# Slot feed-forward: weight units loaded in the order of use, the second bias copied by GpSimd, group outputs sent on the queue of the weight units

## The chip, the cores and the metric

The kernel runs on one core of a Trainium2 chip. The metric is the time of one execution on the device in microseconds; the median of three runs stands for a kernel. Lower is better.

## The reference

Two transformer-like layers run on a batch of B=32 sequences of T=96 tokens (64 image patches and 32 text tokens) of width D=192. Each layer is an attention and a feed-forward, both with residuals. The part that matters here is the feed-forward of layer 0, a mixture over 64 slots: every sequence is gathered into 64 slot vectors, each slot has its own two-layer network with its own weights, and the results are spread back over the tokens.

```python
y = jnp.einsum('btd,bst->bsd', xn, dispatch_w)            # [32, 64, 192]
y = jnp.einsum('sio,bsi->bso', fc1_weight, y) + fc1_bias  # [64, 192, 768] weights
y = jax.nn.gelu(y, approximate=False)
y = jnp.einsum('sio,bsi->bso', fc2_weight, y) + fc2_bias  # [64, 768, 192] weights
out = jnp.einsum('bsd,bst->btd', y, combine_w)            # 64 slots back to 96 tokens
```

All weights are float32. The slot weights alone are 64 x 192 x 768 x 2 values, 75.5 MB, and each is used once, for 32 rows.

## The kernel before

The program is a row of stages, each a `Block` in which the five engines run their own instruction lists, with a barrier at the end: patch embedding, attention 0, slot dispatch, slot feed-forward (`slot_ffn`, L910), combine (L1064), then the second layer. The slot feed-forward, where the change lies, runs at about 342 to 550 us.

**Groups and units.** The 64 slots are worked in NGR=8 groups of GS=8 slots. A group's weights come in PER=4 units of 2304 KB: parts 0 and 1 hold its first-layer weights, parts 2 and 3 its second-layer weights. A unit fills one of NU=6 places of a ring (`g.ring`, 18432 bytes in each of 128 partitions). `load_unit` (L257) loads unit u, which is part `u % 4` of group `u // 4`, into place `u % 6`. The first six units (group 0 complete, and parts 0 and 1 of group 1) are loaded long before, during attention 0.

**TensorE** runs `first(0)`, and then for each group gr: `turn(gr)`, `first(gr+1)`, `second(gr)`. `first` (matmuls of L1028, 96 of them) waits for parts 0 and 1 of its group; `turn` (L1041) transposes the hidden rows; `second` (L1053, 2 x 48 matmuls) waits for part 2 and then for part 3. So TensorE takes the units in the order of groups 0 first, 1 first, 0 second, 2 first, 1 second, and so on. ACT and DVE copy the hidden rows out of PSUM (`evacuate`, L955 and L985), DVE adds the first bias (L992), ACT does the Gelu (L961), and DVE copies a group's output to the two-deep tile `y2g` (`y_copy`, L1001).

**SP** loads units 6 to 31 in the order of their numbers (L938 to L945). Before the load of unit u it waits until the unit that had the place six earlier has been used: `s_h1` counts the halves of `first`, `s_y2p` those of `second`. After unit 6 it also issues one transfer of the second bias, which broadcasts `fc2_b` over the batch into partitions 64 to 127 of `g.y2` (L945): 64 x 32 rows of 192 floats.

**ACT** also issues the group outputs (`put`, L963 to L967): after `y_copy(gr)` two transfers of 96 KB move `y2g` (128 partitions x 192 floats each) to four partitions of `g.y2` of 32 x 192 floats each. `y_copy(gr)` waits until the two transfers of group gr-2 have landed. The stage ends when the last of them has landed, since ACT waits for `s_y2` and the barrier waits for ACT; the combine stage's first matmul (L1080) reads `g.y2`.

Of the kernel before, what the change touches and what calls it, by code (L numbers as in the profile page):

```python
# [24 lines left out]
B = 32  # L25
T_IMG, T_TXT = 64, 32
T = T_IMG + T_TXT
D = 192
# [17 lines left out]
NS = 64  # L46
F = 768
FC = F // 128
GS = 8
NGR = NS // GS  # L50
SC = 4
SH = NS // 2
KQ = D // 64
UNIT = 2 * KQ * F
NU = 6
PER = 4
# [198 lines left out]
    g.b1_rows = hi["b"][64:66, :]  # L255


def load_unit(sp, A, g, u):

    gr, part = u // PER, u % PER  # L260
    src = A["slot_w1"][2 * gr + part] if part < 2 else A["slot_w2"][2 * gr + part - 2]
    sp.dma_start(g.ring[u % NU], src).then_inc(g.s_ring[u % NU], 16)

# [646 lines left out]
def slot_ffn(nc, A, g):  # L910


    with ExitStack() as ctx:
        def sem(name):
            return g.phase_sem("f_" + name)

        def sb(name, shape, dt=F32):
            return ctx.enter_context(nc.sbuf_tensor("f_" + name, shape, dt))

        NCK = 2 * FC  # L920
        N2 = F // 2
        hid = sb("hid", [128, 2, F])
        hT = sb("hT", [128, 2, NCK, 128])
        b1 = sb("b1", [128, NGR, NCK, SC])
        y2g = sb("y2g", [128, 2, 2, D])
        s_b1, s_b2, s_h1, s_hid_a, s_hid_v, s_hTp, s_hb, s_gelu, s_y2p, s_y2s = (
            sem(n) for n in ("b1", "b2", "h1", "hid_a", "hid_v", "hTp", "hb", "gelu", "y2p", "y2s"))
        s_y2 = [sem(f"y2_{i}") for i in range(2)]
        b_h = [[g.ps[:, 2 * n + r, 0:N2] for r in range(2)] for n in range(2)]
        b_hT = [g.ps[:, 4 + q, :] for q in range(3)]  # L930
        b_y = [g.ps[:, 7, r * D:(r + 1) * D] for r in range(2)]
        block = ctx.enter_context(nc.Block())

        @block.sync
        def _(sp):
            sp.dma_start(b1[:, :, :, :], A["slot_b1"].rearrange("p (g k c) -> p g k c", g=NGR, k=NCK)).then_inc(s_b1, 16)
            for u in range(NU, NGR * PER):
                gr, part = (u - NU) // PER, (u - NU) % PER  # L938
                if part < 2:
                    sp.wait_ge(s_h1, 2 * gr + 2)  # L940
                else:
                    sp.wait_ge(s_y2p, 2 * gr + part - 1)
                load_unit(sp, A, g, u)
                if u == NU:
                    sp.dma_start(g.y2[NS:2 * NS, :, :], A["fc2_b"].unsqueeze(1).broadcast_to([NS, B, D])).then_inc(s_b2, 16)  # L945
            sp.wait_ge(s_b2, 16)

        @block.scalar
        def _(act):
            def evacuate(gr):  # L950
                for n in range(2):
                    act.wait_ge(s_h1, 2 * gr + n + 1)
                    if gr >= 1:
                        act.wait_ge(s_hTp, 3 * gr)
                    act.activation(hid[:, 0, n * N2:(n + 1) * N2], b_h[n][0], ACT.Copy).then_inc(s_hid_a, 1)  # L955

            def gelu(gr):
                for q in range(3):
                    act.wait_ge(s_hb, 3 * gr + q + 1)
                    piece = hT[:, gr % 2, 4 * q:4 * q + 4, :]  # L960
                    act.activation(piece, piece, ACT.Gelu).then_inc(s_gelu, 1)  # L961

            def put(gr):  # L963
                act.wait_ge(s_y2s, gr + 1)
                for r in range(2):
                    s0 = SH * r + SC * gr
                    act.dma_start(g.y2[s0:s0 + SC, :, :], y2g[:, gr % 2, r, :]).then_inc(s_y2[gr % 2], 16)  # L967

            evacuate(0)
            for gr in range(NGR):  # L970
                gelu(gr)
                if gr + 1 < NGR:
                    evacuate(gr + 1)
                put(gr)
            for i in range(2):
                act.wait_ge(s_y2[i], 32 * NGR // 2)

        @block.vector
        def _(v):
            def evacuate(gr):  # L980
                for n in range(2):
                    v.wait_ge(s_h1, 2 * gr + n + 1)
                    if gr >= 1:
                        v.wait_ge(s_hTp, 3 * gr)
                    v.tensor_copy(hid[:, 1, n * N2:(n + 1) * N2], b_h[n][1]).then_inc(s_hid_v, 1)  # L985

            def add_bias(gr):
                for q in range(3):
                    v.wait_ge(s_hTp, 3 * gr + q + 1)
                    if gr >= 2:  # L990
                        v.wait_ge(s_y2p, 2 * (gr - 1))
                    v.tensor_tensor(hT[:, gr % 2, 4 * q:4 * q + 4, :].rearrange("p k (c b) -> p k c b", c=SC),  # L992
                                    b_hT[q].rearrange("p (k c b) -> p k c b", k=4, c=SC),
                                    b1[:, gr, 4 * q:4 * q + 4, :].unsqueeze(3).broadcast_to([128, 4, SC, B]),
                                    ALU.add).then_inc(s_hb, 1)

            def y_copy(gr):
                v.wait_ge(s_y2p, 2 * gr + 2)
                if gr >= 2:
                    v.wait_ge(s_y2[gr % 2], 32 * (gr // 2))  # L1000
                v.tensor_copy(y2g[:, gr % 2, :, :], g.ps[:, 7, 0:2 * D].rearrange("p (r d) -> p r d", r=2)).then_inc(s_y2s, 1)  # L1001

            v.wait_ge(s_b1, 16)
            evacuate(0)
            for gr in range(NGR):
                add_bias(gr)
                if gr + 1 < NGR:
                    evacuate(gr + 1)
                y_copy(gr)

        @block.tensor
        def _(pe):
            def landed(u):
                pe.wait_ge(g.s_ring[u % NU], 16 * (u // NU + 1))

            def first(gr):
                landed(PER * gr)
                landed(PER * gr + 1)
                w1 = [g.ring[(PER * gr + i) % NU].rearrange("p (c k f) -> p c k f", c=2, k=KQ) for i in range(2)]
                if gr >= 1:  # L1020
                    pe.wait_ge(s_hid_a, 2 * gr)
                    pe.wait_ge(s_hid_v, 2 * gr)
                for n in range(2):
                    for k in range(KQ):
                        for c in range(SC):
                            for r in range(2):
                                rows = slice(64 * r, 64 * r + 64)
                                mm = pe.matmul(b_h[n][r][B * c:B * (c + 1), :], g.yT[rows, k, SC * gr + c, :],  # L1028
                                               w1[c // 2][rows, c % 2, k, n * N2:(n + 1) * N2],
                                               start=(k == 0), stop=(k == KQ - 1), tile_position=(64 * r, B * c))  # L1030
                    mm.then_inc(s_h1, 1)

            def turn(gr):
                pe.wait_ge(s_hid_a, 2 * gr + 2)
                pe.wait_ge(s_hid_v, 2 * gr + 2)
                for q in range(3):
                    if gr >= 1:
                        pe.wait_ge(s_hb, 3 * (gr - 1) + q + 1)
                    for m in range(4):
                        r, k = (4 * q + m) // FC, (4 * q + m) % FC  # L1040
                        mm = pe.transpose(b_hT[q][:, 128 * m:128 * (m + 1)], hid[:, r, 128 * k:128 * (k + 1)], g.ident[:, :])  # L1041
                    mm.then_inc(s_hTp, 1)

            def second(gr):
                for r in range(2):
                    landed(PER * gr + 2 + r)
                    pe.wait_ge(s_gelu, 3 * gr + 2 + r)
                    if gr >= 1:
                        pe.wait_ge(s_y2s, gr)
                    w2 = g.ring[(PER * gr + 2 + r) % NU].rearrange("p (c k d) -> p c k d", c=SC, k=FC)  # L1050
                    for k in range(FC):
                        for c in range(SC):
                            mm = pe.matmul(b_y[r][B * c:B * (c + 1), :], hT[:, gr % 2, FC * r + k, B * c:B * (c + 1)],  # L1053
                                           w2[:, c, k, :], start=(k == 0), stop=(k == FC - 1), tile_position=(0, B * c))
                    mm.then_inc(s_y2p, 1)

            first(0)
            for gr in range(NGR):
                turn(gr)
                if gr + 1 < NGR:  # L1060
                    first(gr + 1)
                second(gr)
# [789 lines left out]
```

## Time and profile before

| | us |
|---|---|
| median of 3 runs | 1055.19 (1052.2 to 1057.06) |
| profiled execution, its own time | 1051.24 |
| span of the profile | 1049.3 |
| TensorE busy | 794.9 (76%) |
| VectorE / ScalarE / GpSimd busy | 567.0 / 431.8 / 317.9 |
| DMA moved | 119.33 MB, mean 114 GB/s |

The busy share of TensorE over the whole span says little about the stage at 342 to 550 us, which is slices 13 to 20 of the 40 of 26.2 us each (counted from 0): there the digits of DMA stand at 7 to 9 and the bandwidth at 350 to 416 GB/s, while TensorE is half idle. The share of DMA is a mean over 16 DMA engines, so a share of 0.25 is what four engines at work make.

### The profile page before, as it was taken

How to read it: one execution, taken by the hardware profiler on the slowest of the kernel's cores; microseconds unless marked ns; L12 is line 12 of the kernel's file. 1: busy time of each engine (PE TensorE's matmuls, PEld its weight loads, DVE VectorE, ACT ScalarE, POOL GpSimd, SP SyncE). 2: the span in 40 equal slices, each digit the busy share in tenths (PEclk: the TensorE clock that was granted, in tenths of full speed). 3: DMA queues.
4: the chain of work that ended last, by engine and by line, in shares of the span. 5: the costliest groups of instructions: out<-in, count | busy, mean ns of one | idle time of the engine just before them, and what ended most of it. 6: DMA issues, size and time to landing. Idle time of an engine off the chain costs nothing. (4 is left out here: it accounts for less than half of the span.)

```text
span 1049.3 us, 22626 instructions
## 1 busy us (share of the span) xinstructions
PE 794.9 (76%) x7528; PEld 667.3 (64%) x7529; DVE 567.0 (54%) x1402; ACT 431.8 (41%) x1054; POOL 317.9 (30%) x325
## 2 busy tenths in 40 slices
PE   3599999996979624443355998894359999999993
PEld 2378888885968302222234676673349999999993
DVE  2637777777363201111117588886965665556662
ACT  5347676765733201110110467652704444444441
POOL 1311212110032000000000267751774555555552
PEclk9659999998555856676687899996559999999997
DMA  9391000000000799889931900003512333233321
GB/s 283 107 428 51 2 0 0 0 0 1 1 2 2 181 416 370 357 350 367 320 113 32 413 12 1 0 0 99 124 51 42 50 53 53 48 51 52 49 48 19
DMA packets 37999, 119.33 MB, mean 114 GB/s; under 512 B 7538, under 2 KB 28436, under 8 KB 33588
## 3 DMA queue, kind: packets, MB, share of 16 engines
q1 hardware_dynamic: 24980, 104.30, 27.0%
q0 software_dynamic: 10848, 12.67, 7.5%
q10 hardware_dynamic: 2112, 1.57, 0.9%
q8 instruction: 37, 0.61, 0.2%
q14 instruction: 22, 0.18, 0.1%
HBM read 105.77 MB, written 11.14 MB: 111 GB/s over the span
## 5 line engine op out<-in xcount | busy, mean ns | idle before, releaser
L1028 PE MATMUL psum<-flat,m_yT 64*32 64x384 f32 x624 | 47.4, 667 | 102.8 <-issue 101.4
L1645 POOL DMA_INDIRECT out_h<-x_ys,idx x55 | 87.2, 1586 | 100.0 <-ACT x_ys L1670 60.6
L1769 PE MATMUL psum<-w_pairs,x_h_hi 128*128 x330 | 101.7, 370 | 1.1 <-DVE x_h_lo L1697 1.1
L1028 PEld LDWEIGHTS psum<-flat,m_yT 64*32 64x32 f32 x624 | 17.5, 142 | 128.1 <-issue 128.1
L985 DVE COPY f_hid<-psum 128x384 f32<-128x384 f32 x16 | 8.9, 558 | 146.7 <-PE psum L1028 146.7
L1771 PE MATMUL psum<-w_pairs,x_h_lo 128*128 x330 | 82.8, 251 | 0.0
L1697 DVE TENSOR_TENSOR x_h_lo<-psum,x_h_hi 128x384 fp32r<-128x384 f32 x110 | 56.3, 553 | 38.3 <-ACT x_h_hi L1666 37.0
L1221 POOL MEMSET b_ones<- 96x96 f32 x1 | 0.2, 179 | 241.3 <-POOLq L130 241.3
L1670 ACT ACTIVATE x_ys<-x_ys,cw 128x192 f32<-128x192 f32 x55 | 25.1, 456 | 103.0 <-DVE x_ys L1708 103.0
L1769 PEld LDWEIGHTS psum<-w_pairs,x_h_hi 128*128 128x128 f32 x330 | 61.9, 188 | 3.1 <-issue 3.1
L1666 ACT ACTIVATE x_h_hi<-psum 128x384 fp32r<-128x384 f32 x110 | 48.1, 489 | 37.1 <-PE psum L1758 35.3
L1771 PEld LDWEIGHTS psum<-w_pairs,x_h_lo 128*128 128x128 f32 x330 | 62.9, 191 | 0.1
L955 ACT ACTIVATE f_hid<-psum 128x384 f32<-128x384 f32 x16 | 7.9, 491 | 131.5 <-PE psum L1028 131.5
L1632 POOL DMA_INDIRECT x_xg<-xtab,idx x55 | 55.1, 1001 | 16.6 <-issue 14.9
L461 POOL TENSOR_SCALAR a_xn<-flat,rstd,nmr 96x192 f32<-96x192 f32 x32 | 15.9, 498 | 137.1 <-PE psum L592 137.0
L597 PE MATMUL psum<-a_xT,a_wqk 96*96 96x96 f32 x256 | 47.9, 270 | 3.7 <-ACT a_qT L489 1.8
L1326 PE MATMUL psum<-b_wqkv,b_xT 96*96 96x384 f32 x128 | 48.9, 506 | 0.0
L1230 POOL TENSOR_TENSOR b_ra<-b_ra,b_rb 96x384 f32<-96x384 f32 x32 | 31.9, 996 | 55.8 <-DVE b_rb L1180 55.8
L538 DVE TENSOR_REDUCE a_mx<-psum 96x12 f32<-96x1152 f32 x32 | 42.2, 1319 | 12.0 <-PE psum L626 11.9
L1758 PE MATMUL psum<-ident,x_hid 128*128 128x128 f32 x330 | 46.5, 278 | 0.3 <-DVE x_hid L1692 0.3
L633 PE MATMUL psum<-ident,a_p 96*96 96x96 f32 x384 | 44.2, 253 | 2.7 <-ACT a_p L506 2.7
L511 ACT ACTIVATE a_pT<-psum 96x384 f32<-96x384 f32 x96 | 43.4, 483 | 5.3 <-PE psum L633 4.6
(271 smaller groups left out, 2289.2 us busy)
## 6 DMA issues: line engine op xcount, KB each, us to landing
flat<-in_slot_w SPq DMA_DIRECT2D x27, 2304.0 KB, 21.0
ring_last<-in_slot_w SPq DMA_DIRECT2D x5, 2304.0 KB, 26.9
flat<-in_moe_w SPq DMA_DIRECT2D x1, 10752.0 KB, 29.4
flat<-in_x_patches SPq DMA_DIRECT2D x4, 1536.0 KB, 15.0
out_h<-flat SPq DMA_DIRECT2D x1, 2304.0 KB, 12.2
xtab<-flat SPq DMA_DIRECT2D x4, 576.0 KB, 4.0
m_y<-in_fc_b SPq DMA_DIRECT2D x1, 1536.0 KB, 19.5
m_y<-f_y2g ACTq DMA_DIRECT2D x16, 96.0 KB
```

What stands on the lines that cost most here:

```text
L511: act.activation(pT[:, r, :, :], bank_pT[r].rearrange("p (h t) -> p h t", t=T), ACT.Copy).then_inc(s_pTs, 1)
L597: pe.matmul(bank[:, m % 2, :], wqk[0:HALF, 0, m * HALF:(m + 1) * HALF], xT[0:HALF, xk, 0, :], start=True, stop=False)
L633: mm = pe.transpose(bank_pT[r][:, j * T:(j + 1) * T], p[:, i % 2, r * HG + j, :], g.ident[0:T, 0:T])
L1028: mm = pe.matmul(b_h[n][r][B * c:B * (c + 1), :], g.yT[rows, k, SC * gr + c, :], w1[c // 2][rows, c % 2, k, n * N2:(n + 1) * N2], start=(k ...
L1326: mm = pe.matmul(b_qk, xT[:, i % 2, k, :], wqkv[:, k, 0:2 * D], start=(k == 0), stop=(k == 1))
L1632: pool.indirect_dma_start(out=xg[:, t % NX, :], out_offset=None, in_=A["xtab"][:, :], in_offset=bass.IndirectOffsetOnAxis(ap=g.idx[:, t:t ...
L1645: pool.indirect_dma_start(out=A["out"][:, :], out_offset=bass.IndirectOffsetOnAxis(ap=g.idx[:, i:i + 1], axis=0), in_=ys[:, i % 2, :], in_ ...
L1666: act.activation(h_hi[:, 3 * n:3 * n + 3, :], b_hT[n], ACT.Copy).then_inc(s_hh, 1)
L1697: v.tensor_tensor(h_lo[:, 3 * n:3 * n + 3, :], b_hT[n], h_hi[:, 3 * n:3 * n + 3, :].bitcast(F32), ALU.subtract).then_inc(s_hl, 1)
L1758: mm = pe.transpose(b_hT[n][:, k, :], hid[:, c * 128:(c + 1) * 128], g.ident[:, :])
L1769: pe.matmul(b_y[u % 2], h_hi[:, k, :], g.w_pairs[:, :, k, bass.ds(e, 1), :].rearrange("p two a d -> p two (a d)"), start=(k == 0), stop=False)
L1771: mm = pe.matmul(b_y[u % 2][:, 1, :], h_lo[:, k, :], g.w_pairs[:, 1, k, bass.ds(e, 1), :].rearrange("p a d -> p (a d)"), start=False, stop ...
```

## The change

Three edits, all for the slot feed-forward.

1. `load_unit` takes its group and part from a table `ORDER`, which lists the units in the order in which TensorE uses them; TensorE's `landed` looks up a unit's number in the inverse table. The first six units are the same set in another order (units 2 and 3 are now group 1's first-layer weights, units 4 and 5 group 0's second-layer weights). SP's waits follow the same table.
2. The second bias is loaded once per slot (64 rows of 192 floats) into a tile `b2`, before the first weight unit of the stage; GpSimd, which had nothing to do in this stage, copies it with a broadcast over the batch into `g.y2`.
3. `put(gr)` goes from ACT to SP: it stands after the load that takes the place of the group's part 3, and the last groups' after all loads. SP waits for `s_y2` at its end.

```diff
+def use_order():
+    pairs = [(0, 0)]
+    for gr in range(NGR):
+        if gr + 1 < NGR:
+            pairs.append((gr + 1, 0))
+        pairs.append((gr, 2))
+    return [(gr, part + i) for gr, part in pairs for i in range(2)]
+
+ORDER = use_order()
+TURN = {unit: u for u, unit in enumerate(ORDER)}

 def load_unit(sp, A, g, u):
-    gr, part = u // PER, u % PER
+    gr, part = ORDER[u]
     src = A["slot_w1"][2 * gr + part] if part < 2 else A["slot_w2"][2 * gr + part - 2]
     sp.dma_start(g.ring[u % NU], src).then_inc(g.s_ring[u % NU], 16)

@@ slot_ffn
+        b2 = sb("b2", [2 * NS, D])
         @block.sync
         def _(sp):
             sp.dma_start(b1[:, :, :, :], ...).then_inc(s_b1, 16)
+            sp.dma_start(b2[NS:2 * NS, :], A["fc2_b"]).then_inc(s_b2, 16)
+
+            def put(gr):
+                sp.wait_ge(s_y2s, gr + 1)
+                for r in range(2):
+                    s0 = SH * r + SC * gr
+                    sp.dma_start(g.y2[s0:s0 + SC, :, :], y2g[:, gr % 2, r, :]).then_inc(s_y2[gr % 2], 16)
+
             for u in range(NU, NGR * PER):
-                gr, part = (u - NU) // PER, (u - NU) % PER
+                gr, part = ORDER[u - NU]
                 if part < 2:
                     sp.wait_ge(s_h1, 2 * gr + 2)
                 else:
                     sp.wait_ge(s_y2p, 2 * gr + part - 1)
                 load_unit(sp, A, g, u)
-                if u == NU:
-                    sp.dma_start(g.y2[NS:2 * NS, :, :], A["fc2_b"].unsqueeze(1).broadcast_to([NS, B, D])).then_inc(s_b2, 16)
-            sp.wait_ge(s_b2, 16)
+                if part == PER - 1:
+                    put(gr)
+            for gr, part in ORDER[NGR * PER - NU:]:
+                if part == PER - 1:
+                    put(gr)
+            for i in range(2):
+                sp.wait_ge(s_y2[i], 32 * NGR // 2)
+
+        @block.gpsimd
+        def _(pool):
+            pool.wait_ge(s_b2, 16)
+            pool.tensor_copy(g.y2[NS:2 * NS, :, :], b2[NS:2 * NS, :].unsqueeze(1).broadcast_to([NS, B, D])).then_inc(s_b2w, 1)
+            pool.wait_ge(s_b2w, 1)

         @block.scalar
-            def put(gr): ...
             evacuate(0)
             for gr in range(NGR):
                 gelu(gr)
                 if gr + 1 < NGR:
                     evacuate(gr + 1)
-                put(gr)
-            for i in range(2):
-                act.wait_ge(s_y2[i], 32 * NGR // 2)

         @block.tensor
-            def landed(u):
+            def landed(gr, part):
+                u = TURN[gr, part]
                 pe.wait_ge(g.s_ring[u % NU], 16 * (u // NU + 1))
+                return g.ring[u % NU]
```

## Rows read from the trace of the kernel before

**Rows 1.** Page, part 2: tenths in 40 slices of the span.
```profile
PE   3599999996979624443355998894359999999993
...
DMA  9391000000000799889931900003512333233321
GB/s 283 107 428 51 2 0 0 0 0 1 1 2 2 181 416 370 357 350 367 320 113 32 413 12 1 0 0 99 124 51 42 50 53 53 48 51 52 49 48 19
```

**Rows 2.** Waits, 335 to 600 us: who waited for whom, total, times, longest.
```profile
PE psum L1028 <- issue: 101.4, 6, 25.4
```

**Rows 3.** Timeline of TensorE: start, length, instruction, count, idle before it.
```profile
355.37 1.49 PE L1053 MATMUL psum<-flat,f_hT 128*32 128x192 f32 x27
...
360.85 1.53 PE L1041 MATMUL psum<-ident,f_hid 128*128 128x128 f32 x12
387.81 6.21 PE L1028 MATMUL psum<-flat,m_yT 64*32 64x384 f32 x96 [25.43 <-issue]
...
414.32 6.61 PE L1028 MATMUL psum<-flat,m_yT 64*32 64x384 f32 x96 [14.80 <-issue]
...
550.38 14.80 PE L1080 MATMUL psum<-m_y,m_combT 128*96 128x192 f32 x64 [11.19 <-PEq L913]
```

**Rows 4.** Timeline of SP's DMA issues, 335 to 560 us.
```profile
342.03 0.33 SPq L936 DMA_DIRECT2D f_b<-in_slot_b  x1
349.20 0.33 SPq L262 DMA_DIRECT2D flat<-in_slot_w  x1
349.57 0.65 SPq L945 DMA_DIRECT2D m_y<-in_fc_b  x1
```

**Rows 5.** Windows: us, length, busy time (count) of each engine, granted clock, DMA share, GB/s.
```profile
342.00:349.00 7.00, 6.67 (x96) 2.58 (x96) 0.56 (x1) 0.49 (x1) 0.00 (x0) 0.59 0.10 28
350.00:352.00 2.00, 2.00 (x28) 1.50 (x36) 1.43 (x3) 1.70 (x3) 0.00 (x0) 1.00 0.94 240
350.00:366.00 16.00, 11.44 (x216) 7.24 (x216) 5.45 (x9) 5.47 (x9) 0.00 (x0) 0.96 1.07 262
366.00:384.00 18.00, 0.00 (x0) 0.00 (x0) 0.00 (x0) 0.00 (x0) 0.00 (x0) 0.50 1.01 405
400.00:420.00 20.00, 5.68 (x80) 2.35 (x88) 1.13 (x2) 2.12 (x4) 0.00 (x0) 0.57 1.00 424
420.00:424.00 4.00, 4.00 (x104) 2.67 (x92) 0.56 (x1) 0.49 (x1) 0.00 (x0) 1.00 0.28 79
474.00:476.00 2.00, 2.00 (x56) 1.60 (x52) 0.00 (x0) 0.00 (x0) 0.00 (x0) 1.00 0.32 123
534.00:540.00 6.00, 4.11 (x96) 3.65 (x96) 1.05 (x2) 1.50 (x3) 0.00 (x0) 1.00 0.32 34
540.00:546.00 6.00, 0.00 (x0) 0.00 (x0) 0.00 (x0) 0.00 (x0) 0.00 (x0) 0.69 0.27 33
546.00:550.00 4.00, 0.00 (x0) 0.00 (x0) 0.00 (x0) 0.00 (x0) 0.00 (x0) 0.50 0.13 15
```

**Rows 6.** Page, parts 3 and 6: queues (packets, MB, share), issues (KB each, us to landing).
```profile
q10 hardware_dynamic: 2112, 1.57, 0.9%
...
flat<-in_slot_w SPq DMA_DIRECT2D x27, 2304.0 KB, 21.0
...
m_y<-in_fc_b SPq DMA_DIRECT2D x1, 1536.0 KB, 19.5
m_y<-f_y2g ACTq DMA_DIRECT2D x16, 96.0 KB
```

**Rows 7.** Timeline, 525 to 556 us: the last two group outputs.
```profile
532.64 1.15 ACTq L967 DMA_DIRECT2D m_y<-f_y2g  x2
...
539.84 1.15 ACTq L967 DMA_DIRECT2D m_y<-f_y2g  x2
```

**Rows 8.** Groups by line of GpSimd, 560 to 760 us: busy, mean ns.
```profile
L1225 POOL COPY flat<-b_hn 96x192 f32<-96x192 f32 x32 | 12.1, 378 | 9.5 <-DVE b_hn L1201 9.5
```

More of the change, by code:

```diff
@@ L925, in slot_ffn @@
         y2g = sb("y2g", [128, 2, 2, D])
+        b2 = sb("b2", [2 * NS, D])
+        s_b2w = sem("b2w")
         s_b1, s_b2, s_h1, s_hid_a, s_hid_v, s_hTp, s_hb, s_gelu, s_y2p, s_y2s = (
@@ L961, in gelu @@
                     act.activation(piece, piece, ACT.Gelu).then_inc(s_gelu, 1)
[L963 to L967, printed above, removed]
             evacuate(0)
@@ L1012, in _ @@
         def _(pe):
-            def landed(u):
+            def landed(gr, part):
+                u = TURN[gr, part]
                 pe.wait_ge(g.s_ring[u % NU], 16 * (u // NU + 1))
+                return g.ring[u % NU]
             def first(gr):
-                landed(PER * gr)
-                landed(PER * gr + 1)
-                w1 = [g.ring[(PER * gr + i) % NU].rearrange("p (c k f) -> p c k f", c=2, k=KQ) for i in range(2)]
+                w1 = [landed(gr, i).rearrange("p (c k f) -> p c k f", c=2, k=KQ) for i in range(2)]
                 if gr >= 1:
@@ L1045, in second @@
                 for r in range(2):
-                    landed(PER * gr + 2 + r)
+                    w2 = landed(gr, 2 + r).rearrange("p (c k d) -> p c k d", c=SC, k=FC)
                     pe.wait_ge(s_gelu, 3 * gr + 2 + r)
@@ L1049, in second @@
                         pe.wait_ge(s_y2s, gr)
-                    w2 = g.ring[(PER * gr + 2 + r) % NU].rearrange("p (c k d) -> p c k d", c=SC, k=FC)
                     for k in range(FC):
```

## Prediction

> **What bounds the kernel now.** I read the slices first, then the waits of the stage, then TensorE's timeline with SP's, and last windows cut to the bursts and the gaps. The slices show that at 342 to 550 us, where the edits lie, the DMA engines are full and TensorE is not [rows 1]. The waits name it: 101.4 us in six waits ahead of L1028, the first-layer matmuls, put down to issue, that is, to nothing an engine did, which with weights in flight means a weight unit that had not landed [rows 2]. In the timeline the idle 25.43 us ahead of 387.81 is the largest: `first(2)` needs group 2's parts 0 and 1, which SP sends only after group 1's parts 2 and 3 and after the bias [rows 3, 4].
>
> This looks like a matter of order: in each group TensorE works, places come free late, and the bandwidth drops for some us (79 GB/s at 420 to 424, 123 at 474 to 476), while between the gaps it stands at 424 [rows 5]. But the same windows show something else. The DMA share in the gaps is never near zero: 0.28, 0.32, and after the last weights 0.32 and 0.27 with 34 and 33 GB/s [rows 5]. 0.27 of 16 engines is 4.3. And ACT's queue, which carries only the group outputs, has 2112 packets for 1.57 MB: 16 transfers of 96 KB in rows of 768 bytes are 2048, and the 64 left over are four for each transfer [rows 6]. So a group output is carried by four DMA engines, each with a row of 32 packets for one destination partition as I read it, and these four have something to do in every gap. I take it that they are the same four each time: two outputs in hand at once (issued at 532.64 and 539.84 [rows 7]) never raise the share to eight engines' 0.5. If so, the stage is bounded not by the bandwidth of 16 engines and not by the order, but by the sum of the work of those four: their sixteenths of each weight unit, of the bias, and a quarter of each output.
>
> The Trainium skill, "DMA: Bandwidth & Descriptors", section "Why a DMA increments its semaphore by 16 and not by 1", says that a transfer from SP or ACT is split over the largest number of engines up to 16 that divides the slowest dimension on both sides, and takes the lowest-numbered of them. By it an output uses four engines, always the same, whether ACT or SP issues it. The packet count above agrees; that it is the same four no row here shows by itself.
>
> **The account of the four engines before.** From the first unit's issue at 349.20 [rows 4] to L1080 at 550.38 [rows 3] are 201.2 us.
> - 26 weight units: 2304 KB are 2.359 MB, at 424 GB/s 5.56 us each, 144.7 us.
> - Start: 350 to 352 moved 240 GB/s, 0.9 us short of full, and 0.8 us lie between 349.2 and 350: 1.7 us.
> - The bias: 350 to 366 moved 16 x 262 GB/s = 4.19 MB [rows 5]. Less its own 1.57 MB, 2.62 MB of weights moved, 6.2 us of the 16. With the start's 0.9 out, it cost 8.9 us, and 366 to 384 at 405 instead of 424 adds 0.8. I take 9.5 us.
> - End: 546 to 550 has half the share of the windows before it, so the outputs end near 548 to 549.5; 1 us for the last landing and the barrier.
> - What is left, 44.3 us, is eight pairs of outputs: 5.5 us a pair.
>
> A check on that: two pairs alone on the engines, 534 to 546, ran at 33.5 GB/s, and a pair of 197 kB is then 5.9 us [rows 5]. The four engines thus have no idle time to give back.
>
> **The change, part by part.**
> *Order of the units.* It removes the gaps of the other twelve engines. `first(2)` needs the first two units sent: they land at 349.2 + 1.7 + 11.1 = 362.0, where TensorE ends `turn(1)` at 362.4, instead of 387.8 [rows 3]. But the stage still ends when the four engines are through, so this alone gives nothing. It costs nothing either: SP's queue must not run dry on the four. At the start two units (11.1 us) are queued at 349.2; the next two need `first(1)`, which ends at 355.4 [rows 3], 5 us before the queue is dry. Later, when a group's first-layer weights land, four more units are queued and `first` takes 6.6 us at most [rows 3].
>
> *Second bias.* The 1536 KB transfer goes (−9.5 us on all 16 engines). In its place 48 KB are issued right behind L936's transfer at 342.03 [rows 4], where the share is 0.10 until 349 [rows 5]: by the price of the old one 0.3 us, hidden in that gap. GpSimd's copy is 6144 elements a partition; its copy of 192 took 378 ns [rows 8], so 12.1 us, from about 345 to 357. Cover is the whole stage to 540; without it, it would cost those 12.1 us. It could delay DVE's copies beside it at 349 to 357, which have the 5 us of slack named above.
>
> *Outputs on SP's queue.* ACT loses 16 issues and the waits ahead of them; ACT is not late anywhere, so 0. SP gains eight waits on `y_copy`, each about 1 us after the load ahead of it is allowed. Queued behind is the next load, whose place comes free only after the next `first`: 0. An output now stands behind up to six units, 33 us, in place of being taken in turn with them. `y_copy(gr+2)` waits for it, but needs two more units after that, so 11 us of slack; only `y_copy(7)` may wait, for the output of group 5, with that of group 6 still in the queue to cover it. The last outputs stand after the last weights as before.
>
> The one price that no row shows is a pair's cost in a row between weights, not in turn with them. Low bound: the bias's packets, also 768 bytes and also in SP's queue, 128 on each engine for 9.5 us, 0.074 us each; a pair is 64 on each of the four, 4.75 us. High: a pair alone, 5.9 us, plus the 0.8 us lost after the bias, once for each of the two transfers, 7.5 us. A price near zero is in the rivals. I take the 5.5 us of the account, since the packets, engines and partitions are the same ones.
>
> **Sum.** 349.2 + 1.7 + 144.7 + 8 x 5.5 (44.3) + 1.0 = 540.9, against 550.4: 9.5 us less, just the bias. On the profiled execution's 1051.24 that is 1041.7. The median of the runs is 3.95 above it; I put the 9.5 on the median of 1055.19: **1045.7 us**. By the bounds of the pair: 4.75 gives 534.6 (15.8 less, 1039.4), 5.9 gives 543.8 (6.6 less, 1048.6).
>
> **Rivals.**
> 1. *Outputs cost nearly nothing in the queue* (all 16 engines carry them, or their packets hide behind weights). For it: while an output is under way beside weights, the bandwidth stays at 424 GB/s [rows 5]. Against: the shares of 0.27. Then the last weights land at 349.2 + 1.7 + 144.7 = 495.6, plus some 5 for five pairs, half of `second(7)` 2.1, copy 0.6, last pair 3: about 507, 43 less. If five pairs hide and the last three cost 5.9: 349.2 + 1.7 + 144.7 + 17.7 + 1 = 514.3, 36 less. I use **1015 us**. The same page of the Trainium skill, section "Anatomy of one DMA", fits a transfer as 2.0 us plus bytes over 436 GB/s, by which an estimate for a pair in a full queue is 0.45 us; it would land here.
> 2. *Same within the measurement*: a pair costs 5.9 to 7.3 us in a row, since nothing lies between its packets to hide the wait for each; 543.8 to 555, **1051 us** at 6.2.
> 3. *Slower*: each output is a stall in the weights' own queue. One pair costs 5.9 + 2 x 0.8 = 7.5 us (high bound): 349.2 + 1.7 + 144.7 + 60 + 1 = 556.6, 6.2 us more, **1061 us**. It decides from 6.7 us a pair on, (44.3 + 9.5)/8. For it: in turn with weights a small packet hides, in a row it does not.
> 4. *The order was the bound after all*, and the four engines' work is small: same time as 1.
>
> **How the numbers follow.** Forecast (pair 4.7 to 5.9) 0.47; rival 2 0.29; rival 3 0.12; rivals 1 and 4 together 0.12. Within 0.5% (5.3 us) is about what a measurement of this kernel can tell from no change. Faster: 0.47 + 0.12 = 0.59; same 0.29; slower 0.12. The range 1030 to 1058 leaves out half or so of rival 3 and all of 1; it takes in the forecast's bounds and partial hiding.
>
> **What would show it.** Gaps of twelve engines gone early, `first(2)` at about 362 and `first(3)` at about 385; then TensorE's `first` spaced by 4 x 5.56 + 5.5 = 27.8 us, not by 22.3; that of group 7 at about 495; last weights landed near 523, then 17 us with a share of 0.27 until L1080 at about 541. No L945 on SP, a GpSimd copy of 12 us. If `first` is spaced by 22 us, rival 1 or 4 holds; by 29 or more, rival 3. If the share falls near zero in any gap, the four engines were not the bound.

## The result

| | before | changed |
|---|---|---|
| median | 1052.47 (20 runs) | 1054.82 (20 runs) |
| span of the profile | 1049.3 | 1054.7 |
| slot feed-forward, first weight issue to the combine stage's first matmul | 201.2 | 204.3 |

The ratio is 1.0025 with a 95% interval of 1.0013 to 1.0037: the changed kernel is 2.3 us slower, by under the 0.5% that the prediction called no change. Forecast were 9.5 us less. With twenty runs the median of before is 1052.47, 2.7 below the three runs shown; the comparisons with before below go by ratios or by medians taken side by side.

SP's and GpSimd's timelines of the changed kernel (start, length, instruction) show the edits in place: the bias is a small transfer ahead of the weights, and the copy takes 5.3 us, not 12.1.

```profile
344.62 0.33 SPq L952 DMA_DIRECT2D f_b<-in_slot_b  x1
345.00 0.47 SPq L953 DMA_DIRECT2D f_b<-in_fc_b  x1
351.41 9.39 SPq L276 DMA_DIRECT2D flat<-in_slot_w  x5
```

```profile
347.37 5.30 POOL L979 COPY m_y<-f_b 64x6144 f32<-64x6144 f32 x1 [13.33 <-DMA f_b<-in_fc_b]
```

TensorE's timeline of the changed kernel, which answers to [rows 3]:

```profile
366.46 5.80 PE L1053 MATMUL psum<-flat,m_yT 64*32 64x384 f32 x96 [2.62 <-issue]
...
390.29 0.86 PE L1053 MATMUL psum<-flat,m_yT 64*32 64x384 f32 x4 [7.81 <-issue]
...
419.42 6.72 PE L1053 MATMUL psum<-flat,m_yT 64*32 64x384 f32 x96 [7.24 <-issue]
...
507.91 6.85 PE L1053 MATMUL psum<-flat,m_yT 64*32 64x384 f32 x96 [6.39 <-issue]
...
555.73 14.80 PE L1104 MATMUL psum<-m_y,m_combT 128*96 128x192 f32 x64 [14.20 <-PEq L927]
```

`first(2)` starts at 366.46 in place of 387.81, and the 25.43 us of idle ahead of it are 2.62. But from 390.29 to 507.91, four groups on, `first` comes every 29.4 us; in the kernel before it was 26.5 (387.81 to 414.32), and 27.1 over the same four groups. The lead of 21 us is spent group by group. Where, the windows of the changed kernel show (columns as in [rows 5]):

```profile
376.00:386.00 10.00, 5.06 (x60) 3.36 (x60) 2.43 (x4) 1.82 (x3) 0.00 (x0) 0.83 1.01 425
388.00:392.00 4.00, 1.71 (x24) 0.77 (x32) 0.00 (x0) 0.00 (x0) 0.00 (x0) 0.50 1.02 112
418.00:422.00 4.00, 2.58 (x35) 1.06 (x43) 0.00 (x0) 0.00 (x0) 0.00 (x0) 0.50 1.05 124
448.00:452.00 4.00, 3.83 (x49) 1.55 (x57) 0.00 (x0) 0.00 (x0) 0.00 (x0) 0.50 1.12 123
478.00:482.00 4.00, 3.77 (x48) 1.52 (x56) 0.00 (x0) 0.00 (x0) 0.00 (x0) 0.50 0.94 132
...
536.00:554.00 18.00, 2.16 (x48) 1.46 (x48) 0.56 (x1) 0.00 (x0) 0.00 (x0) 0.73 0.25 40
```

At 376 to 386 weights run at 425 GB/s with a DMA share of 1.01. At 388 to 392 the share is still 1.02, and 112 GB/s move. This comes back once a group. The engines are all busy and carry a quarter: it is not four engines at work with twelve idle, which would be a share of 0.27 as in the gaps of before, but sixteen engines held up. Twelve of them have no packet of the output, by the packet count of [rows 6], and are slow all the same. I call it the jam. The last line is the end: the last weights' rest and three pairs of outputs, on four engines (0.25).

### The profile page after: what moved, and what is told of

The parts are those of the page before. It is cut to its first block and busy times, and to the rows that moved or that the text cites. A ratio compares the mean times of both kernels' runs of the same rounds, so it can differ in the third digit from the quotient of the medians.

```text
span 1054.7 us, 22627 instructions
## 1 busy us (share of the span) xinstructions
PE 813.1 (77%) x7528; PEld 673.8 (64%) x7529; DVE 566.8 (54%) x1402; ACT 433.4 (41%) x1054; POOL 323.7 (31%) x326
## 3 DMA queue, kind: packets, MB, share of 16 engines
q1 hardware_dynamic: 25108, 104.35, 28.4%
## 5 line engine op out<-in xcount | busy, mean ns | idle before, releaser
L1077 PE MATMUL psum<-flat,f_hT 128*32 128x192 f32 x624 | 42.0, 436 | 44.9 <-DMA flat<-in_slot_w 44.8
L1077 PEld LDWEIGHTS psum<-flat,f_hT 128*32 128x32 f32 x624 | 24.3, 144 | 63.5 <-DMA flat<-in_slot_w 51.5
L1026 DVE COPY f_y2g<-psum 128x384 f32<-128x384 f32 x8 | 4.5, 558 | 93.8 <-PE psum L1077 81.9
L995 ACT ACTIVATE f_hT<-f_hT 128x512 f32<-128x512 f32 x24 | 14.6, 629 | 92.1 <-DVE f_hT L1017 92.1
## 6 DMA issues: line engine op xcount, KB each, us to landing
flat<-in_moe_w SPq DMA_DIRECT2D x1, 10752.0 KB, 29.4
```

## The experiments

All were timed beside the kernel before; the medians of before were 1052.47 beside the changed kernel, then 1052.64 (order_only to order_bias), 1052.52 (after_spread to slot_by_slot), 1051.48 (after_spread8 to before_spread) and 1053.52 (before_no_outputs). "Stage" is the span from the first weight issue to the combine stage's first matmul, from each run's timelines.

| run | median | to before | stage |
|---|---|---|---|
| changed kernel | 1054.82 | +0.25% | 204.3 |
| order_only | 1044.92 | −0.71% (0.9907 to 0.9952) | 195.2 |
| bias_only | 1044.70 | −0.75% (0.9902 to 0.9948) | 193.2 |
| queue_only | 1072.35 | +1.89% (1.0163 to 1.0215) | 223.1 |
| order_bias | 1037.43 | −1.40% (0.9833 to 0.9886) | 188.9 |
| after_spread | 1029.86 | −2.20% (0.9766 to 0.9793) | 180.2 |
| order_bias_spread | 1026.26 | −2.47% (0.9739 to 0.9768) | 176.2 |
| no_outputs | 1012.23 | −3.86% (0.9599 to 0.9630) | 161.8 |
| slot_by_slot | 1058.81 | +0.52% (1.0031 to 1.0073) | 211.5 |
| after_spread8 | 1028.86 | −2.23% (0.9750 to 0.9804) | 177.8 |
| order_bias_spread8 | 1025.47 | −2.51% (0.9722 to 0.9777) | 176.6 |
| after_step2 | 1032.56 | −1.79% (0.9788 to 0.9855) | 182.1 |
| before_spread | 1035.79 | −1.61% (0.9807 to 0.9872) | 185.3 |
| before_no_outputs | 1030.39 | −2.25% (0.9725 to 0.9826) | 181.8 |

### The three edits one by one

order_only and bias_only are the kernel before with the first and the second edit of the diff. queue_only has the third on top of before's order:

```diff
                 load_unit(sp, A, g, u)
+                if part == PER - 1:
+                    put(gr)
+            for gr in range((NGR * PER - NU) // PER, NGR):
+                put(gr)
```

order_bias is the changed kernel without the third edit, with `put` back on ACT.

> The kernel before with the units in the order of use alone. Theory A (the sum of the work of the four DMA engines that carry the outputs is the bound; the order gives nothing by itself): within 2 us of the kernel before. Rival C (without gaps in the weights the outputs on ACT's queue only trickle, one small packet for each weight packet, and y_copy comes to wait for them): 3 to 12 us slower, with idle time ahead of y_copy ended by an output transfer. Rival D (the order was the bound): 20 us or more faster.

> The kernel before with the second bias loaded once and copied by GpSimd, nothing else. Theory A: the 9.5 us of the 1536 KB transfer go from all 16 DMA engines, 7 to 10 us faster. Rival B (the bias lay beside work that bounds anyway): within 2 us.

> The kernel before with the group outputs issued by SP behind the load that takes the place of part 3, nothing else. Theory A (in a row between weights the small packets slow the weight packets of all 16 engines, 7.2 us a pair against the 5.5 of the account): 8 x 1.7 = 11 to 14 us slower. Rival B (the queue hardly matters): within 3 us.

> The changed kernel with the group outputs back on ACT's queue (order and bias copy kept). Theory A: 7 to 10 us faster than before, so 9 to 12 faster than the changed kernel. Rival B (the queue hardly matters and the bias was worth little): like the changed kernel, within 3 us of it. Rival C (outputs trickle on ACT's queue once the weights have no gaps): slower than the changed kernel.

Measured against before: order −7.7 us, bias −7.9, queue +19.7, order and bias together −15.2. The first two add up, and the third, on top of them, costs 1054.8 − 1037.4 = 17.4 us. So the change is 15 us of gain and 17 us of loss. Theory A had the bias right. It had the sign of the queue right and the size too small (11 to 14 expected). It gave the order nothing and was wrong there by 7.7 us, well outside its 2, and so also in order_bias (15.2 us against 7 to 10). Rival B falls with bias_only and queue_only. Rival D (20 us or more from the order) falls too. Rival C is half right: in order_bias the waits of 345 to 545 us have the one that it foresaw,

```profile
DVE f_y2g L1021 <- DMA m_y<-f_y2g: 70.0, 3, 34.6
```

`y_copy` waiting 70 us in three waits for outputs that trickle beside the weights (57.8 us in two waits in order_only), but the time is better all the same. Windows of order_bias, beside an output under way and in the hole that such a wait tears:

```profile
384.00:400.00 16.00, 9.08 (x144) 4.13 (x144) 1.11 (x2) 2.65 (x5) 0.00 (x0) 0.68 1.00 419
464.00:470.00 6.00, 0.00 (x0) 0.00 (x0) 0.00 (x0) 0.00 (x0) 0.00 (x0) 0.50 0.24 87
```

419 GB/s while group 0's outputs are under way, issued at 360.85 and landed only when `y_copy(2)` could start at 414.12: from a queue of their own they did not jam the weights here, as I read it because they take turns with them. That is not so everywhere. In the kernel before, also with the outputs on ACT's queue, the weights come in bursts, and where a burst starts together with an output, issued at 504.93, the window shows a jam:

```profile
506.00:508.00 2.00, 0.00 (x0) 0.00 (x0) 0.78 (x2) 1.67 (x3) 0.00 (x0) 1.00 1.19 129
```

The second bias was a jam as well. In before_no_outputs (below), which has the old bias transfer in the weights' queue and no output at that time:

```profile
360.00:362.00 2.00, 1.81 (x21) 1.29 (x12) 1.58 (x3) 0.23 (x1) 0.00 (x0) 1.00 1.14 188
```

It writes the same small rows to 64 partitions, so a jam does not need a place of only four; bias_only has 429 GB/s at 358 to 362.

In queue_only, with the outputs in SP's queue, the window from 384 has the jam again:

```profile
384.00:388.00 4.00, 0.00 (x0) 0.00 (x0) 0.00 (x0) 0.00 (x0) 0.00 (x0) 0.50 1.07 121
```

### What jams: the place written to, or the four engines

after_spread gives a group other slots. The weights are laid out to match; packets, bytes, queues and the four engines stay the same (SP's queue has 25,108 packets in both).

```diff
-                                mm = pe.matmul(..., g.yT[rows, k, SC * gr + c, :],
+                                mm = pe.matmul(..., g.yT[rows, k, NGR * c + gr, :],
-                    sp.dma_start(g.y2[s0:s0 + SC, :, :], y2g[:, gr % 2, r, :])
+                    sp.dma_start(g.y2[SH * r + gr:SH * (r + 1):NGR, :, :], y2g[:, gr % 2, r, :])
```

order_bias_spread is the same with ACT's queue. slot_by_slot keeps the neighbouring partitions and takes all 16 engines, with 64 issues in place of 16. SP's queue then has 26,068 packets: the 960 more are 64 x 16 − 16 x 4, one for each engine that takes part in a transfer, as in [rows 6].

```diff
+                    for c in range(SC):
+                        s = SH * r + SC * gr + c
+                        sp.dma_start(g.y2[s:s + 1, :, :], y2g[B * c:B * (c + 1), gr % 2, r, :])
```

no_outputs leaves out the outputs of groups 0 to 6 of the changed kernel, and with them the wait of `y_copy` on them; its result is incomplete.

> The changed kernel with another choice of slots for a group: slots gr, gr+8, gr+16, gr+24 of each half instead of four neighbours, so that an output transfer has the same four DMA engines, packets and bytes but writes to partitions 8 apart instead of 4 neighbouring ones. Theory P (the price of an output, and the collapse of the weights to 110 to 130 GB/s beside it, come from all its packets going to one narrow group of destination partitions): a pair falls from 7.1 us to 2.5 to 4, 25 to 35 us faster than the changed kernel, and no window of high DMA share under 300 GB/s. Rival Q (it is the small packets and the four engines, wherever they write): within 4 us of the changed kernel.

> Order of use, bias copy, outputs on ACT's queue, and the output partitions 8 apart. Theory P: 10 to 20 us faster than order_bias (1037.4), near 1020 to 1027, since the outputs that drain alone in the gaps go faster. Rival Q: within 4 us of order_bias.

> The changed kernel without the output transfers of groups 0 to 6 (only group 7's are sent; the rows of the others are left at zero, so the feed-forward's result is missing there). It gives the whole price of the outputs. By the account 8 pairs cost 57 us in the changed kernel, so 7 fewer give a stage of about 155 to 160 us instead of 204: 1005 to 1012 us. Rival (the weights themselves are slower than 5.56 us a unit, and the outputs only fill what is idle): 1030 us or more.

> The changed kernel with each output transfer cut into four, one for each slot: 32 rows of 768 bytes from 32 partitions into one partition, carried by all 16 engines in place of four. Theory P (destination partitions are the limit): no gain, 0 to 15 us slower than the changed kernel, all bytes still go to the same narrow place, one partition at a time. Rival Q (the work of four engines is the limit): each engine has a quarter of the packets, 30 to 40 us faster.

after_spread is 25.0 us faster than the changed kernel and slot_by_slot not faster (4.0 us slower by the medians, 2.8 by the ratios, whose intervals overlap). Same engines and other partitions: 25.0 of the 42.6 us that the outputs cost (no_outputs, below) are gone. Four times the engines and the same partitions: nothing gained. The 64 issues are not what cost slot_by_slot its gain: SP ended group 3's eight issues at 446.48 and sent the next weights only at 459.92, when a place was free. Theory P stands and rival Q falls, in both directions. With the outputs on ACT's queue the spread brings 11.2 us (order_bias_spread against order_bias), inside the 10 to 20 expected; and between after_spread and order_bias_spread the queue makes 3.6 us where it made 17.4. In after_spread the expectation was too bold: its 25 to 35 us were met at the edge, and the windows at an output still fall under 300 GB/s, to 264 here and to 231 at 466 to 470,

```profile
386.00:390.00 4.00, 2.06 (x32) 0.93 (x40) 0.00 (x0) 0.00 (x0) 0.00 (x0) 0.52 1.11 264
```

while slot_by_slot stands at 160 over 8:

```profile
384.00:392.00 8.00, 0.00 (x0) 0.00 (x0) 0.00 (x0) 0.00 (x0) 0.00 (x0) 0.64 1.11 160
```

Without the outputs the weights flow at 427 GB/s from 376 to 492, `first` comes every 22.0 us (once 23.5), and 42.6 us are gone (1012.2, just outside the 1005 to 1012 expected, and far from the rival's 1030): seven pairs cost 6.1 us each in the changed kernel.

```profile
376.00:492.00 116.00, 72.81 (x1056) 40.77 (x1060) 18.07 (x30) 14.12 (x25) 0.00 (x0) 0.72 1.01 427
```

The Trainium skill, "SBUF — State Buffer", section "Door 1: The DMA port swizzle", says that four neighbouring partitions, and the four that lie 32 further, share one of 16 DMA ports of about 27 GB/s. By it both transfers of a pair, to 4gr and 32 + 4gr, go through one port, partitions 2 apart through two and partitions 8 apart through four. The runs agree in kind, and in size too: the pair of group 7 in no_outputs, alone on the engines, moved at 25 GB/s after 61 in its first us,

```profile
506.00:508.00 2.00, 0.00 (x0) 0.00 (x0) 0.00 (x0) 0.00 (x0) 0.00 (x0) 0.54 0.31 25
```

and the 33 GB/s of [rows 5] are a mean over 12 us with two groups' pairs and their faster starts. The Trainium skill, "DMA: Bandwidth & Descriptors", section "Back-pressure in remote DMA", has the other half, told there of transfers between cores: a saturated destination port clogs the path back to the source engines. The jam of weights that go elsewhere looks like it, within one core; no run here shows the path itself.

### How wide the place is

after_spread8 and order_bias_spread8 shift the second half's partitions by 4 against the first half's; after_step2 takes partitions 2 apart; before_spread is the kernel before with partitions 8 apart. The first three share this edit, with STEP 8 or 2:

```diff
+def first_slot(gr, r):
+    return (gr + 4 * r) % NGR            # STEP = 8
+    return 8 * (gr // 2) + gr % 2        # STEP = 2
-                    s0 = SH * r + SC * gr
+                    s0 = SH * r + first_slot(gr, r)
+                    ... g.y2[s0:s0 + (SC - 1) * STEP + 1:STEP, :, :] ...
```

> The changed kernel with output partitions 8 apart, and the second half's shifted by 4 against the first half's: each output transfer still writes to four partitions 8 apart, but the two of a pair no longer to the same rows of eight. Theory P, narrow reading (a group of destination partitions p//4 modulo 8 shares one way in, and the two transfers of a pair meet there): 4 to 12 us faster than after_spread (1029.9), since each engine goes on to fresh partitions. Theory P, wide reading (partitions 8 apart are already enough, what is left is the work of four engines, about 4 us a pair): within 3 us of after_spread.

> The same on top of order_bias_spread (outputs on ACT's queue, 1026.3 us). Wide reading: within 3 us of it. Narrow reading: 3 to 10 us faster.

> The changed kernel with output partitions 2 apart (four partitions within eight, so two neighbourhoods of four in place of one; after_spread has four). If a neighbourhood of four partitions is one way in, two of them halve the jam: between the changed kernel (1054.8) and after_spread (1029.9), 1032 to 1045. If the distance of 8 itself is what helps, like the changed kernel, above 1050. If any gap between the partitions is enough, like after_spread, under 1032.

> The kernel before with the output partitions 8 apart, nothing else. Theory P: a pair falls from 5.5 us by the account to about 3.6 as in order_bias_spread, 8 x 1.9 = 15 us less, 1034 to 1042, unless the order of the units now bounds (then under 8 us less, and the four engines idle in the gaps: a window of share under 0.1).

The shift brings 1.0 and 0.8 us by the medians, 0.3 and 0.4 by the ratios, less than the intervals: the wide reading. Call partitions 4k to 4k + 3 a neighbourhood. Partitions 2 apart, in two neighbourhoods, bring 22.3 of the 25.0 us, at the lower edge of "two of them halve the jam" and 0.6 us from "any gap is enough", so the time alone does not tell these two apart. The traces do, in the last pair, alone on the engines: after_step2 and before_spread,

```profile
527.00:529.00 2.00, 0.00 (x0) 0.00 (x0) 0.00 (x0) 0.00 (x0) 0.00 (x0) 0.50 0.30 48
```

```profile
531.00:534.00 3.00, 0.00 (x0) 0.00 (x0) 0.00 (x0) 0.00 (x0) 0.00 (x0) 0.74 0.23 66
```

One neighbourhood moved 25 GB/s (no_outputs), two 48, four 66, all on four engines at a share of 0.23 to 0.31. The rate doubles with the second neighbourhood, so the neighbourhoods count and not any gap; from two to four it no longer doubles, which fits the four engines as the next limit, but no run tests that. Partitions 4 apart and a place of two adjacent partitions were not run either. before_spread comes out at 1035.8, 15.7 us less, as the 8 x 1.9 of the expectation. order_bias_spread8, 1025.5 us, is the fastest here, 26 us (2.5%) under before, though not apart from order_bias_spread (0.4 us by the ratios).

### Why the order gained

before_no_outputs leaves out the outputs of groups 0 to 6 in the kernel before, as no_outputs does in the changed one.

> The kernel before without the output transfers of groups 0 to 6 (only group 7's are sent, the other rows of the feed-forward's result stay zero). Open is why the order of the units alone gave 7.7 us where the account gave it nothing. Theory S (the order by itself costs nothing; it only decided whether outputs meet weights in bursts and jam them): only the bias stands between this and no_outputs (1012.2), so 1018 to 1023. Rival O (with the order of before the weights' queue itself runs dry in every group, outputs or not): 1027 or more, with windows of DMA share under 0.15 in each group.

1030.4 us, so rival O by its time: 18.2 us above no_outputs, of which the bias is 8 if it costs as much as in bias_only, and some 10 are left for the order alone; no run has the order alone without outputs. Its other sign, windows under 0.15 in each group, is not there; the shortfall is smaller and comes once a group, as at 391 to 395, where `second(1)` (started at 391.81) has to free places before SP can issue:

```profile
391.00:395.00 4.00, 4.00 (x104) 2.73 (x92) 0.56 (x1) 0.49 (x1) 0.00 (x0) 1.00 0.66 271
```

TensorE's timeline around it:

```profile
384.93 6.95 PE L1035 MATMUL psum<-flat,m_yT 64*32 64x384 f32 x96 [23.11 <-issue]
391.81 4.11 PE L1060 MATMUL psum<-flat,f_hT 128*32 128x192 f32 x96
...
408.44 5.44 PE L1035 MATMUL psum<-flat,m_yT 64*32 64x384 f32 x96 [11.07 <-issue]
```

The next load is issued only at 394.02. `first` comes every 23.5 us (the third line less the first) with the order of before and no outputs, every 22.0 with the new order. And seven pairs cost 23.1 us in before, 3.3 each, against 6.1 in the changed kernel. That part of their work ran in the holes that the order tore is my reading of the shares of 0.28 to 0.32 there; no run separates it from the queue.

## Why the prediction was wrong

*The four engines.* Right as an observation: outputs ran on four engines, with the share of 0.27 in the gaps [rows 5]. Wrong as the bound. "The four engines thus have no idle time to give back" took a busy engine for a working one. What they waited for was the place that they wrote to: before_spread, with the same engines, packets and bytes, is 15.7 us faster, the share of ACT's queue, which carries only the outputs, falls from 0.9% to 0.5%, and slot_by_slot, with four times the engines, gained nothing. The sign named for this case, a share near zero in some gap, could not show it, because an engine held up counts as busy.

*The account.* "What is left, 44.3 us, is eight pairs of outputs: 5.5 us a pair" gave the price that was carried over. The remainder was made of two things, the outputs and the order, that lay partly on top of each other. Measured, a pair was worth 3.3 us in before and the order some 10 us without outputs (18.2 less the bias), 7.7 with them. The check with the pairs alone at the stage's end (5.9 us) seemed to confirm it, but a pair alone is not a pair beside weights.

*Order, 0 us.* Measured −7.7. "But the stage still ends when the four engines are through, so this alone gives nothing" was false: in before the weights' queue did come short once a group, with or without outputs.

*Second bias, −9.5.* Measured −7.9, inside the 7 to 10 of the expectation. The copy took 5.3 us, not 12.1, and lay in the stage as foreseen.

*Outputs on SP's queue, 0 us.* This is the step that failed: "I take the 5.5 us of the account, since the packets, engines and partitions are the same ones". It gave the move to SP's queue no price, and the runs showed +17.4 us on top of the other two edits and +19.7 on the kernel before, some 2.2 us a pair. By the same account the changed kernel has (204.3 − 147.4) / 8 = 7.1 us a pair, queue_only (223.1 − 156.9) / 8 = 8.3; with the outputs taken away a pair is worth 6.1 us in the changed kernel and 3.3 in before. The sum priced the time of the four engines that carry an output. What came in its place is the jam: all 16 engines, those with weights alone too, move 112 to 132 GB/s for some us in each group.

The rivals came nearer. 7.1 us lies in rival 2's 5.9 to 7.3 and past the 6.7 from which rival 3 decides; the two overlap there. By the time, 2.3 us slower and within 0.5%, rival 2 holds. Rival 3 named the sign to look for, `first` spaced by 29 or more, and it is 29.4. Its mechanism, "in turn with weights a small packet hides, in a row it does not", holds as far as it goes; the jam of all 16 engines was not in it. Its 1061 put a pair at 7.5 us, and at 7.1 eight pairs are 3.1 us less. Rival 1's price of 0.45 us a pair is far from all runs; the lowest is 2.0 us, in order_bias_spread ((1026.3 − 1012.2) / 7). `y_copy(7)` did wait for group 5's output, 11.8 us, as the text said.

*In all*: the order and the bias gave 15.2 us, the queue took 17.4. The forecast had 0, 9.5 and 0. That the measured 1054.82 lies inside the range of 1030 to 1058 is luck as far as the working goes: two terms put at nothing, −7.7 and +17.4, partly cancel.

## What to carry to other kernels

A transfer that gathers many partitions into a few neighbouring ones was slow for what it moved, and placed in a row in the queue of the large loads it slowed them all here: look for windows with a full DMA share and a fraction of the bandwidth. Choose the numbering so that the rows written together lie apart, which here cost only another layout of the weights; that alone turned the three edits from 2.3 us slower into 22.7 faster. A queue of their own brought 17.4 us while the rows lay together, and 3.6 once they lay apart. An account that puts the whole remainder on one cause needs a run that takes this cause away, before its price is carried to another place.

## What the runs showed of the hardware

- 16 DMA engines at a share of 1.02 moved 112 GB/s while an output of 197 kB ran in the weights' queue, against 425 without one (376 to 386 us).
- Alone on four engines, an output to adjacent partitions moved 25 GB/s after its first us (no_outputs), to partitions 2 apart 48, 8 apart 66.
- The same output with its four destination partitions 8 apart in place of adjacent: a stage of 180.2 us against 204.3. With partitions 2 apart 182.1.
- Spreading each output over 16 engines, one destination partition at a time: a stage of 211.5 us.
- The bias's broadcast transfer of 1.57 MB to 64 partitions, in the weights' queue: 188 GB/s at a share of 1.14 (before_no_outputs).
- On another queue an output beside an unbroken row of weights did not lower their 419 GB/s, but had to trickle: group 0's took 53 us from issue to landing, and `y_copy` waited up to 34.6 us for one. With partitions 8 apart (order_bias_spread) the longest wait was 34.1, so the place is not what makes it trickle. Where a burst of weights began with the output, it was 129 GB/s at a share of 1.19 (before).
- GpSimd's broadcast copy of 64 x 6144 float32 took 5.3 us, 0.86 ns an element of a partition, while a copy of 192 took 378 ns [rows 8]. At 0.86 ns its 192 elements would be 165 ns, so by this estimate more than half of the small copy is fixed cost.
